# Two gated attention and mixture-of-experts layers: scores made four heads at a time, and loops written out

## The reference

```python
for layer in (0, 1):
    n = layernorm(x)                                   # x: (8, 100, 512), float32
    q, k, v = n @ wq + bq, ctx @ wk + bk, ctx @ wv + bv   # ctx: (8, 722, 512), 16 heads of 32
    s = q @ k.T / sqrt(32)                             # layer 0: masked keys get -1e9
    x = x + tanh(g_xattn[layer]) * ((softmax(s) @ v) @ wo + bo)
    n = layernorm(x).reshape(800, 512)
    if layer == 0:                                     # 64 experts, 8 a token, at most 256 tokens each
        y = swiglu(n; shared 1024) * sigmoid(n @ sg) + sum_k w_k * swiglu_expert(n; 256)
    else:                                              # 8 experts, 2 a token
        y = gelu_mlp(n; shared 2048) + sum_k w_k * gelu_mlp_expert(n; 2048)
    x = x + tanh(g_ffn[layer]) * y
```

## Time and profile before

| what | value |
|---|---|
| median of 3 runs | 2503.39 us (2495.83 to 2504.03) |
| the profiled execution's own time | 2507.09 us |
| its span, mean granted clock | 2505.3 us, 0.929 |
| TensorE, its weight load | busy 2253.1 us (90%), 1581.1 us (63%) |
| VectorE, ScalarE, GpSimd | 1216.8 (49%), 936.2 (37%), 535.5 (21%) |
| DMA | 287.89 MB, fastest of the page's 40 slices 344 GB/s |
| zeroing of the sums | three DMAs of 2048 KB, one of 256 KB |
| attention of layer 0, of layer 1 (second blocks) | 53 to 594 us, 1317 to 1850 us |
| routing to the experts' first load, layer 0 | 596 to 810 us |
| experts of layer 0 | 810 to 1250 us |
| routing, layer 1; its experts | 1852 to 2074 us; 2076 to 2490 us |

### The profile page before, as it was taken

How to read it: one execution, slowest core, us unless ns; L and a number is a source line. 1 busy time by engine, 2 the same in 40 slices (tenths; PEclk the granted TensorE clock), 3 DMA queues, 4 the chain that set the end, 5 groups by cost and what they waited for, 6 DMA issues and landing times. The chain is left out here.

```text
span 2505.3 us, 39432 instructions
## 1 busy us (share of the span) xinstructions
PE 2253.1 (90%) x13564; PEld 1581.1 (63%) x13565; DVE 1216.8 (49%) x2072; ACT 936.2 (37%) x1523; POOL 535.5 (21%) x574
## 2 busy tenths in 40 slices
PE   6899999987893899999848999999869997999995
PEld 4777777765861444444427777777659535777773
DVE  3466666654722222222264666666533014777776
ACT  2355555543110111111112555555433104656663
POOL 0000000001375455445400000000012301232321
PEclk9899999985896899999968999999858998999997
DMA  4300000003000999999630100000030005756652
GB/s 155 133 30 30 30 30 30 1 1 131 1 1 22 334 319 344 317 335 286 155 147 29 37 32 25 25 25 1 1 132 1 34 0 220 279 216 213 244 186 65
DMA packets 64805, 287.89 MB, mean 115 GB/s; under 512 B 11740, under 2 KB 12142, under 8 KB 45354
## 3 DMA queue, kind: packets, MB, share of 16 engines
q1 hardware_dynamic: 42842, 246.40, 26.2%
q0 software_dynamic: 21840, 39.69, 7.4%
HBM read 257.85 MB, written 33.96 MB: 116 GB/s over the span
## 5 line engine op out<-in xcount | busy, mean ns | idle before, releaser
L582 ACT ACTIVATE probs<-ps,stat 100x722 f32<-100x722 f32 x256 | 219.3, 862 | 152.4 <-DVE stat L519 76.0
L1214 PE MATMUL pgu<-ring,xT 128*128 x560 | 267.5, 601 | 6.5 <-issue 2.4
L434 PE MATMUL pt<-ident,probs 100*128 100x100 f32 x1536 | 194.3, 266 | 50.2 <-ACT pTs L570 49.2
L570 ACT ACTIVATE pTs<-pt 128x600 f32<-128x600 f32 x256 | 171.9, 671 | 114.2 <-PE pt L434 108.3
L434 PEld LDWEIGHTS pt<-ident,probs 100*128 100x128 f32 x1536 | 158.5, 149 | 86.2 <-DVE probs L507 45.7
L1214 PEld LDWEIGHTS pgu<-ring,xT 128*128 128x128 f32 x560 | 100.2, 192 | 114.0 <-issue 113.6
L507 DVE TENSOR_SCALAR probs<-probs,stat 100x722 f32<-100x722 f32 x256 | 157.6, 616 | 9.1
L1571 DVE TENSOR_TENSOR ws_low<-w,ws_high 128x2048 fp32r<-128x2048 f32 x63 | 142.9, 2291 | 24.1 <-ACT ws_high L1502 24.1
L1260 ACT ACTIVATE sg<-pgu 128x256 f32<-128x256 f32 x70 | 26.9, 384 | 313.2 <-PE pgu L1214 313.2
L1228 PE MATMUL pd<-ring,hT 128*128 x280 | 132.7, 596 | 1.7 <-issue 0.8
L519 DVE CUSTOM_DVE_ANT_0 ps<-ps,madd 100x722 f32<-100x722 f32 x128 | 114.1, 933 | 36.0 <-PE ps L425 36.0
(11 more groups left out here) (252 smaller groups left out, 5084.5 us busy)
## 6 DMA issues: line engine op xcount, KB each, us to landing
ring<-in_l_ew SPq DMA_DIRECT2D x64, 1536.0 KB, 8.8
w<-in_l_ew SPq DMA_DIRECT2D x64, 1024.0 KB, 8.0
xnT<-in_ctxT SPq DMA_DIRECT2D x14, 1444.0 KB, 7.0
wu<-in_l_up SPq DMA_DIRECT2D x2, 4096.0 KB, 12.6
b<-in_l_eb SPq DMA_DIRECT2D x8, 1024.0 KB, 4.7
moe_sum<-zrow SPq DMA_DIRECT2D x3, 2048.0 KB, 13.4
moe<-moe_sum SPq DMA_DIRECT2D x24, 200.0 KB
wd<-in_l_down SPq DMA_DIRECT2D x2, 2048.0 KB, 11.6
```

Of the source, the lines that this page charges most:

```text
L434: last = pe.transpose(pt[:, kc // 3, (kc % 3) * S:(kc % 3 + 1) * S], probs[s % 4][:, kc * P:(kc + 1) * P], ident[0:S, 0:S])
L570: act.activation(pTs[:, g % 2, s % HPC, :, :].rearrange("k (a c) q -> k a (c q)", a=2), pt[:, :, 0:3 * S], ACT.Copy).then_inc(t_out, 1)
L582: act.activation(probs[s % 4][:, 0:SK], scores_of(s), ACT.Exp, bias=stat[:, s, 1:2], scale=-1.0 if masked else 1.0, accum_out=stat[:, s, 2 ...
L1214: last = pe.matmul(pgu[p][:, :], xT[p][:, c, :], wgu[c], start=c == 0, stop=c == DC - 1)
```

## The change

Keys are cut in segments of 362 and 360. Scores of a half step are those of four heads (one group) for one segment, in four bands of 32 rows and four PSUM tensors of one bank. Each segment has its own maximum; the exponentials of a segment are taken against it (half as wide, twice as many), and six small operations a group on VectorE and one exponential on ScalarE make the factor of each segment by which its half of the probabilities is normalised. Transposes trail by a group. Eight tiles of probabilities of 722 keys replace four of 768, the transposes of the tail chunk have 82 keys. The loops of the attention over batches on TensorE, VectorE and ScalarE are written out. The output bias is scaled and added to x by GpSimd in the first block, where the zeroing of the sums goes too; masks are loaded straight to their place.

In the routing the casts of constants on VectorE move ahead of the wait for the logits, `chosen`, `ones` and `before` get f32r copies, and 17 f32r matmuls on broadcast operands replace 88 f32 ones. GpSimd scatters without copies, written out. `slot_indices` goes: SyncE loads the table in the routing's block, TensorE transposes it after the down product, VectorE copies it. TensorE's loop over expert pairs is written out for pairs 1 to 30 and loops on from 31.

```diff
-SEG = ((0, 512), (512, SK))
+SEG = ((0, 362), (362, SK))
...
+                    pool.wait_ge(bo_in, 16)
+                    pool.tensor_scalar(bo[:, :], bo[:, :], env.gate[0:S, layer:layer + 1], None, ALU.mult)\
+                        .then_inc(bo_scaled, 1)
+                    pool.wait_ge(bo_scaled, 1)
+                    for t in range(B):
+                        pool.tensor_tensor(x[:, t, :], x[:, t, :], bo[:, :], ALU.add).then_inc(x_biased, 1)
...
+        ps = [cx.enter_context(nc.psum_tensor(env.name(f"ps{n}"), [P, 512], F32)) for n in range(HPC)]
...
+        BESIDE = {4: (("k", 0, 0), ("k", 0, 1)), 5: (("k", 1, 0), ("k", 1, 1)), 6: (("k", 2, 0), ("k", 2, 1)),
+                  7: (("v", 0), ("v", 1)), 8: (("k", 3, 0), ("k", 3, 1)), 9: (("v", 2), ("v", 3)),
+                  10: (("v", 4), ("v", 5)), 11: ()}
...
-        def over_batches(engine, body):
-            with engine.Fori(0, B // 2 - 1) as i:
-                for p in range(2):
-                    body(i * 2 + p, p, 2)
-            for p in range(2):
-                body(B - 2 + p, p, 1 - p)
+        def over_batches(body):
+            for b in range(B):
+                body(b, b % 2, min(2, B - 1 - b))
...
+                def scores(b, p, g, seg, first=False):
+                    if g == 0 and seg == 0:
                         pe.wait_ge(q_ready, b * 2 + 2)
-                    if i % 2 == 0:
-                        ready = max(PIECES.index(("k", c, 0)), PIECES.index(("k", c, 1)))
-                        pe.wait_ge(piece_out, b * NPIECE + ready + 1)
+                    pe.wait_ge(piece_out, b * NPIECE + (PIECES.index(("k", g, seg)) + 1))
                     if not first:
-                        pe.wait_ge(exp_done, b * H + 2 * i)
-                    for k0, k1 in SEG:
-                        for x, y in PARTS:
-                            for s in (2 * i, 2 * i + 1):
-                                rows = slice(s % HPC * DH, (s % HPC + 1) * DH)
-                                last = pe.matmul(ps[s % 2][0:S, k0:k1], qb[p][x][rows, c, :], kT[y][rows, c, k0:k1],
-                                                 start=(x, y) == PARTS[0], stop=(x, y) == PARTS[-1])
+                        pe.wait_ge(exp_done, b * (2 * H) + (g * 2 + seg) * HPC)
+                    k0, k1 = SEG[seg]
+                    for x, y in PARTS:
+                        for j in range(HPC):
+                            rows = slice(j * DH, (j + 1) * DH)
+                            last = pe.matmul(ps[j][0:S, 0:k1 - k0], qb[p][x][rows, g, :], kT[y][rows, g, k0:k1],
+                                             start=(x, y) == PARTS[0], stop=(x, y) == PARTS[-1])
                     last.then_inc(s_mm, 1)
...
+                    for h in HALVES:
+                        if h < NHALF or left:
+                            scores(*at_half(b, p, h))
+                        tb, _, tg, late = at_half(b, p, h - 2)
+                        turn = h < NHALF + 2 or left
+                        pieces = BESIDE[h] if left else ()
+                        if h % 2 == 0:
+                            weighted_values(b, p, h // 2 - 2, left)
+                        if pieces:
+                            piece(pieces[0])
                         if turn:
-                            transposed(tb, 2 * ti)
-                        for what in items:
-                            item(what)
+                            transposed(tb, tg, 2 * late)
+                        if pieces:
+                            piece(pieces[1])
+                        if h == HALVES[-1]:
+                            outputs(b, left)
                         if turn:
-                            transposed(tb, 2 * ti + 1)
-                    pe.wait_ge(ao_ready, b * NG + NG)
-                    for c in range(DC):
-                        last = pe.matmul(po[0:S, :], aoT[:, c, :], wo[:, c, :], start=c == 0, stop=c == DC - 1)
-                    last.then_inc(o_mm, 1)
-                over_batches(pe, body)
+                            transposed(tb, tg, 2 * late + 1)
+                over_batches(body)
...
+                def segments_apart(b, g):
...
+                    dve.tensor_tensor(least[:, g, :], less_max[:, g, 0, :], less_max[:, g, 1, :], ALU.min)\
+                        .then_inc(least_done, 1)
...
+                    dve.tensor_tensor(apart[:, g, :, :], least[:, g, :].unsqueeze(1).broadcast_to([S, 2, HPC]),
+                                      less_max[:, g, :, :], ALU.subtract).then_inc(apart_done, 1)
+                def factors(b, g):
+                    n = b * NG + g + 1
...
+                    dve.tensor_tensor(factor[:, g, :, :], share[:, g, :, :], sums[:, g, :, :], ALU.mult)\
+                        .then_inc(weighed, 1)
...
+                    dve.tensor_tensor(total[:, g, :], factor[:, g, 0, :], factor[:, g, 1, :], ALU.add)\
+                        .then_inc(total_done, 1)
...
+                    dve.reciprocal(over[:, g, :], total[:, g, :]).then_inc(over_done, 1)
...
+                    dve.tensor_tensor(factor[:, g, :, :], share[:, g, :, :],
+                                      over[:, g, :].unsqueeze(1).broadcast_to([S, 2, HPC]), ALU.mult)\
+                        .then_inc(factor_done, 1)
...
+                def normalised(g, j):
+                    for seg, (k0, k1) in enumerate(SEG):
+                        at = probs[g % 2 * HPC + j][:, k0:k1]
+                        dve.tensor_scalar(at, at, factor[:, g, seg, j:j + 1], None, ALU.mult).then_inc(norm_done, 1)
...
+                    for h in HALVES:
+                        bb, bp, g, seg = at_half(b, p, h)
+                        _, _, tg, late = at_half(b, p, h - 2)
+                        pieces = BESIDE[h] if left else ()
+                        if h < NHALF or left:
+                            maxima(bb, bp, g, seg)
+                            if seg == 1:
+                                segments_apart(bb, g)
+                        if seg == 0 and (h < NHALF + 2 or left):
+                            normalised(tg, 2)
+                            normalised(tg, 3)
+                        for what in pieces[:1]:
+                            piece_rest(dve, what, b + 1, 1 - p)
+                        if seg == 1 and (h < NHALF or left):
+                            factors(bb, g)
+                        if h == HALVES[-1]:
+                            residual()
+                        if seg == 1 and (h < NHALF or left):
+                            normalised(g, 0)
+                            normalised(g, 1)
+                        for what in pieces[1:]:
+                            piece_rest(dve, what, b + 1, 1 - p)
+                        if left == 2:
+                            for part in {10: (0, 1), 11: (2,)}.get(h, ()):
+                                split_low(dve, b + 2, part)
+                over_batches(body)
...
+                    for h in HALVES:
+                        bb, bp, g, seg = at_half(b, p, h)
+                        tb, _, tg, late = at_half(b, p, h - 2)
+                        lb, _, lg, l_late = at_half(b, p, h - 3)
+                        pieces = BESIDE[h] if left else ()
+                        if h < NHALF + 3 or left:
+                            turned(lb, lg, 2 * l_late + 1)
+                        active = h < NHALF or left
+                        if active:
+                            exponents(bb, g, seg, (0, 1))
+                        if h % 2 == 0:
+                            heads_out(b, h // 2 - 2)
+                        elif pieces:
+                            piece_high(act, pieces[0], b + 1)
+                        if active:
+                            exponents(bb, g, seg, (2, 3))
+                            if seg == 1:
+                                shares(bb, g)
+                        if pieces and h % 2 == 0:
+                            piece_high(act, pieces[0], b + 1)
+                        if h < NHALF + 2 or left:
+                            turned(tb, tg, 2 * late)
+                        for what in pieces[1:]:
                             piece_high(act, what, b + 1)
...
+                def exponents(b, g, seg, heads, first=False):
+                    k0, k1 = SEG[seg]
+                    for j in heads:
+                        if not first:
+                            act.wait_ge(t_mm, b * H + (g * HPC + j - 7))
+                        act.wait_ge(max_ready, b * (2 * H) + ((g * 2 + seg) * HPC + j + 1))
+                        act.activation(probs[g % 2 * HPC + j][:, k0:k1], ps[j][0:S, 0:k1 - k0], ACT.Exp,
+                                       bias=less_max[:, g, seg, j:j + 1], scale=-1.0 if masked else 1.0,
+                                       accum_out=sums[:, g, seg, j:j + 1]).then_inc(exp_done, 1)
+                def shares(b, g):
+                    act.wait_ge(apart_done, b * NG + g + 1)
```

(48 more changed lines are left out.)

505 lines of the change are left out of this document (236 added, 269 removed).

## The result

The changed kernel takes 2412.23 us (median of 4 executions, 2408.26 to 2416.45), the kernel before 2503.71 (4 executions, 2495.83 to 2507.68): a ratio of 0.964, 95% interval 0.961 to 0.967. The forecast was 2372, the range 2330 to 2435. So it lies in the range, 40 us above the forecast, and 7 above the upper end of the likeliest case. The profiled execution took 2411.5 us with a span of 2409.7; against the profiled execution of before that is 95.6 us of span saved where the sum has 135.

The account below looks back on a forecast made before the run. TensorE's issue bounds full batches, a three-engine chain the last ones, GpSimd layer 0's routing, TensorE the experts. Terms -49 - 36 - 3 - 1.4 - 30 - 14 - 2 = -135 from 2507.1 give 2372 us, range 2330 to 2435.

Parts of the forecast that it names:

- the likeliest case: Whole kernel: the prediction's own sum of 2372 us, bounds 2345 to 2405, chance 0.65.
- Full batches: Attention, seven full batches in two layers: 61.5 to 58.0 us each, 3.5 less, together -49 us (bounds -70, +4).
- I count that gone: Full attention batches: TensorE's 0.9 us wait per batch for a copied transpose disappears, as transposes trail a four-head group.
- Last batches: Last batch of each attention: 43 us against 60.9, -18 a layer, -36 together (bounds -10 and -50).
- The start of attention: First pieces and steps mixed with scores: -3 us in layer 0, 0 in layer 1 (bounds -10, +8).
- Writing the batches out removes back edges; ... I give it nothing: Attention loops: 0 us, since batches with a back edge inside last 61.3 to 61.6 us like those without.
- Routing, layer 0: Layer 0's routing: fewer matmuls, earlier GpSimd, scatters without copies, table loaded within the block; -30 us (bounds -20, -38).
- Routing, layer 1: Layer 1's routing: 17 matmuls for 88 give -11.5, table load and wait go; -14 us (-8, -17).
- two by two (1): Attention scores: bands overlap only in pairs, so scores give nothing; -82, 2425 us, chance 0.10.
- one by one (3): Attention scores: four heads' bands don't overlap at all, 2.15 us a half step; 2549 us, chance 0.03.
- (2): Within a batch: three-engine chain takes over, VectorE's in-order waits delay each half by 1 us; 2484 us, chance 0.10.
- (4): TensorE faster than thought: clock full in the last batches, no waits at the values; 2335 us, chance 0.12.

Follow-up runs that it names:

- e9: e1 with VectorE's low split of the next context but one moved behind the last half step's maxima; 2400.6 us, ratio 0.961.
- e12: e2's GpSimd copies and waits ahead of each eight scatters, plus e9's order of VectorE's low splits; 2390.42 us, ratio 0.955.
- e10: Kernel before, with only the first six batches of each attention written out on TensorE, VectorE and ScalarE; 2498.69 us, ratio 0.999.
- e7: Changed kernel with the first six batches of each attention back in a hardware loop on TensorE, VectorE and ScalarE; 2440.13 us, ratio 0.973.
- e1: Changed kernel, but GpSimd waits for the scatters' semaphore and raises another once, for which SyncE waits; 2386.33 us, ratio 0.955.
- e2: Changed kernel with GpSimd's two small copies and the wait for them back ahead of each eight scatters; 2396.45 us, ratio 0.958.
- e3: Kernel before, with SyncE also waiting within the routing block on the two semaphores the scatters raise; 2502.58 us, ratio 1.0007.
- e4: Changed kernel, but ScalarE waits on the scatters' semaphore and raises another once, for which SyncE waits; 2388.38 us, ratio 0.954.

## Why the prediction was right or wrong, step by step

**Full batches: the scores right, a wait that didn't go.** Between the first output product and the last but one lie six batches a layer; they lost 15.1 and 11.6 us, 26.7 where the forecast has 12 x 3.5 = 42. The scores are as forecast. "0.50, and the same edges as now ...: 0.67 us" is what a half step takes with a piece behind it, 0.67 to 0.68; the values wait 0.21 us four times a batch for the 0.3 of the forecast. Eight half steps take 6.6 us, forecast 5.4 and 1.2. (The Trainium skill, "TensorE: Matmul & The Clock Gate", Part 3, Measured speedup vs the span model, led me to an estimate of 0.82 for its 3.07 times. The trace does not agree: 0.82 is only the mean of eight half steps with their waits, and without a wait one takes 0.67.) The step that failed is "I count that gone". TensorE's wait of 0.9 us a batch for a copied transpose did not go: it is 1.1 us now and stands behind the output product, because VectorE's low split of 2.35 us holds up the last half's maxima. e9 and e12 show this cause by taking it away: 0.8 to 1.0 us a batch. And layer 1 had no such wait to lose: over six of its batches before, 1425.5 to 1789, the view of TensorE's waits has 0.2 us in all, and afterwards 1.0 us a batch stand there too. So layer 0 has some 2.9 and 0.9 less and 1.1 more, 2.5 by the distances, and layer 1 2.7 less and 1.0 more, 1.9 by the distances. A third slip hid that: "layer 1 is the same within 0.1 us" came from a stretch of 61.5 us laid over batches of 60.65; a stretch shows its own width.

**Last batches: right.** 16.4 and 19.2 us less, 36 in all, as forecast (44.35 and 41.74 us for 43; in the runs with the same code they took 44.3 to 46.2 and 42.8 to 44.8, so a fit to the microsecond is luck). Residual: 1.5 for 1.4. The start of attention with the first batch in it: 4.7 us less in layer 0 where 6.5 were due, 9.0 in layer 1 where 3.5 were; within the bounds of +8 and -10 each. Together that is 3.7 us more than was due, which I can't explain, and it hides as much of the 15 that the full batches lack.

**"Writing the batches out removes back edges; ... I give it nothing": the number came out, the reason didn't hold.** e10 confirms it for the kernel before. But with the new schedule a loop costs 28 us (e7), so the sum of -135 could not have been had with the loops kept. I had cited the Trainium skill ("Runtime: NRT & Kernel Launch", Instruction fetch mechanics): a taken branch that leaves the window stalls until its page is fetched. In e7 the trace agrees, with 3.6 us without a releaser ahead of the first matmuls behind the back edge, but no run shows that it is the fetch; in the kernel before it doesn't show. Why the old order hides it was not tried.

**Routing, layer 0: the failed step.** "The 64 scatters show 67.4 us busy and 24.3 idle ...; the copies between them go, leaving ... 87 for 95: -8.5". The scatters did gain, 10.2 us (82.5 from the first start to the last instead of 92.7; the forecast's own "87 for 95" is 8.0, not 8.5), GpSimd starts 13.4 us earlier (17 forecast; the products take 3.7 us and the wait for `chosen` shrank by 1.4 only), and the table load lies beside the end of the block: without late increments the stage is 27.2 us shorter (e1), against 30. What failed is the assumption that the copies were pure cost. With the pauses they made (before, e2, e3, e10, e12) no increment was late; without them VectorE hears, in seven kernels of nine, of TensorE's tiles late, in the changed kernel by up to 45 us, and 24 of the 27 us go back. No rival of mine had it; I had weighed GpSimd only for its own time.

**Routing, layer 1: right; experts: too small to tell.** 17 products between 1822.84 and 1824.4, 1.6 us; -13.3 for -14. The scatters end before TensorE needs anything of them there. Experts -3.0 for -2, less than the spread of that stage.

The rivals: four bands start as one, so neither two by two (1) nor one by one (3); VectorE is at 74% with 43.9 us, forecast 44, and TensorE waits for a copied transpose, 1.3 us a batch, not 1 us in every half (2); the clock is 0.65 and 0.71 in the last batches and the values do wait (4). So 2412 us came by none of them. Of the 40 us between forecast and time 12 are attention's and 27 the first routing's, 24 of these by late increments, which no term and no rival had; that the time lies in the range all the same is the width of the range, not foresight.

**What stays open.** What exactly holds the increments back, and how it hangs together with the missing records; why e1 and e4 had none late in eight executions and e9, with e1's routing, had a slight case in its profiled execution and, by their times, a full one in the other five; and whether six or four scatters in a row would be better than eight.
